# One-hot matrices by groups of 8 rows, two groups at a time, chunk innermost

## What is computed

```python
edge_index = jnp.stack([src, dst])
x = _layernorm(x + _L0_gnn_ref(x, src, dst, edge_weight, ...))   # relu(segment_sum(w * (x W)[dst], src) + b)
x = _layernorm(x + _L1_gnn_ref(x, edge_index, ...))              # 4-head attention over edges, softmax per dst
x = _layernorm(x + _L2_gnn_ref(x, ...))                          # attention over the same edges
x = _layernorm(x + _L3_gnn_ref(x, edge_index, ...))              # two mean aggregations over edges
```

## Time and profile before

| | us |
|---|---|
| median of 3 runs (2888.77 to 2893.41) | 2890.57 |
| profiled execution, its own time | 2890.26 |
| its span, first to last instruction | 2888.6 |
| edge tables, about | 0 to 66 |
| building of the matrices, about | 66 to 888 |
| the four layers | 888 to 2889 |

### The profile page before, as it was taken

The page is one execution under the profiler, slowest core; times in us unless marked ns, Lnnn a source line. Parts: engine busy times, 40 slices in busy tenths (PEclk is TensorE's granted clock), DMA queues, the critical chain, the costliest instruction groups (busy, mean ns, idle before and its releaser), DMA issues. The chain is left out here.

```text
span 2888.6 us, 62252 instructions
## 1 busy us (share of the span) xinstructions
PE 2395.0 (83%) x16954; PEld 1630.4 (56%) x16955; DVE 2073.9 (72%) x3472; ACT 1727.9 (60%) x4122; POOL 473.1 (16%) x825
## 2 busy tenths in 40 slices
PE   1898999889988958888888888888739999959795
PEld 1444444445544546666666666666617888835453
DVE  6776777777771025999999999999467888566075
ACT  1898999999992015766677777666426666410101
POOL 0444444444441000000000000000000000001010
PEclk7999999999999978999999999999869999979897
DMA  1222222222227801222222222222123333058193
GB/s 40 96 102 99 104 98 104 104 101 107 100 103 291 303 18 74 73 87 92 93 93 93 93 93 93 93 93 72 53 82 125 113 121 129 3 247 344 46 426 126
DMA packets 132234, 341.18 MB, mean 118 GB/s; under 512 B 13957, under 2 KB 114936, under 8 KB 115704
## 3 DMA queue, kind: packets, MB, share of 16 engines
q1 hardware_dynamic: 131960, 338.62, 31.5%
HBM read 212.41 MB, written 126.18 MB: 117 GB/s over the span
## 5 line engine op out<-in xcount | busy, mean ns | idle before, releaser
L434 PE MATMUL ps_build<-OH,KEY 128*128 128x400 bf16 x4108 | 737.4, 339 | 82.9 <-ACT KEY L391 47.2
L391 ACT ACTIVATE KEY<-KEY,cols 128x128 bf16<-128x128 bf16 x2054 | 621.7, 397 | 101.1 <-DVE KEY L362 100.0
L434 PEld LDWEIGHTS ps_build<-OH,KEY 128*128 128x128 bf16 x4108 | 399.8, 99 | 420.9 <-DVE OH L366 85.9
L1078 ACT ACTIVATE exponentials<-gr_ps,att_cols 128x256 f32<-128x256 f32 (+1 forms) x1300 | 499.5, 487 | 192.9 <-PE gr_ps L972 190.6
L362 DVE TENSOR_SCALAR KEY<-iota_key,key_base,cols 128x128 bf16<-128x128 int16 x1027 | 389.9, 412 | 220.9 <-PE ps_build L434 193.8
L409 POOL TENSOR_TENSOR KEY<-KEY,cols 128x256 bf16<-128x256 bf16 (+1 forms) x627 | 376.5, 601 | 499.6 <-DVE KEY L362 499.6
L972 PE MATMUL gr_ps<-ident,gr_r 128*128 128x128 f32 x2500 | 382.0, 292 | 84.3 <-DVE gr_r L1186 67.4
L1193 DVE SCALAR_TENSOR_TENSOR exponentials<-exponentials,gr_count_t 128x3072 f32<-128x3072 f32 (+1 forms) x104 | 349.4, 3360 | 54.2 <-ACT gr_count_t L1095 37.6
L1001 PE MATMUL gr_ps<-exponentials,heads 128*33 128x128 f32 x5000 | 366.1, 278 | 26.7 <-DVE exponentials L1193 26.7
L972 PEld LDWEIGHTS gr_ps<-ident,gr_r 128*128 128x128 f32 x2500 | 283.9, 147 | 168.7 <-issue 135.5
L1159 DVE CUSTOM_DVE_ANT_0 gr_unread<-gr_src_rows,gr_closed 128x3125 bf16<-128x3125 f32 (+1 forms) x100 | 344.1, 3441 | 13.5 <-ACT gr_closed L1071 12.9
(11 more groups left out here) (273 smaller groups left out, 1976.6 us busy)
## 6 DMA issues: line engine op xcount, KB each, us to landing
adjacency<-stage SPq DMA_DIRECT2D x200, 400.0 KB, 2.5
sage_ring<-count_by_source SPq DMA_DIRECT2D x50, 1600.0 KB, 9.2
agg_gcn_ring<-adjacency SPq DMA_DIRECT2D x25, 1600.0 KB, 8.3
gr_count<-adjacency SPq DMA_DIRECT2D x25, 1600.0 KB, 7.8
ar_counts<-adjacency SPq DMA_DIRECT2D x25, 1600.0 KB, 6.7
count_by_source<-gr_count_t SPq DMA_DIRECT2D x12, 3200.0 KB, 18.8
fg_node<-gat_node_sums SPq DMA_DIRECT2D x1, 1650.0 KB, 6.3
count_by_source<-gr_count_t SPq DMA_DIRECT2D x1, 1600.0 KB, 7.1
```

What stands on the lines that cost most here:

```text
L391: last = act.activation(KEY[:, slot + j, v, :], KEY[:, slot + j, 0, :], ACT.Copy, scale=k.cols[:, 1 + v, bass.ds(c + j, 1)])
L434: last = pe.matmul(ps[:, 2 * (s % 2) + (v > 0), 0:SL], KEY[:, slot + j, v, :], OH[:, slot + j, :], start=slot == s % 2 * (BODY + 1) and j ...
L1078: last = act.activation(e[:, s, 0:w], ps[:, i % RINGS, c:c + w], ACT.Exp, bias=cols[:, h, s:s + 1])
```

## The change

WD becomes 8 and SL 200, so a window has 8 rows x 16 slabs = 128 keys, and there are 400 windows. They are done two at a time: 200 pairs. A window's body is 3 chunks, a pair's six (BOTH). Buffers have four slots of a pair (RING), guarded the same way at each pair, and the loop has 50 laps of four.

- POOL no longer multiplies. It gathers, for each pair, the six chunks' keys (less the window's base), low parts and two weight parts as bf16 into `near`, and the third weight part as fp32 into `last_w`: three instructions for each window.
- VectorE makes KEY for all six chunks in one tensor_tensor of 128 x 6 against a grid, OH in one of 200 x 6, and then multiplies KEY by the first and second weight part, in two more. The chunk is the innermost index of all of them: KEY is [P, RING, 4, 128, 6].
- ScalarE multiplies by the third part, in six ACTIVATEs that read and write every sixth element, and copies four banks of 200 columns.
- TensorE's matmuls have 200 columns, and read KEY and OH with a step of six elements. Four a chunk, as before.
- A window's fourth chunk, and any behind it, go to a single extra slot, made wholly by VectorE behind its branch; TensorE takes it between the pair's first four chunks and its last two.
- SyncE stores counts and weights apart, in two DMAs a pair.
- `edge_tables` makes the slab number with three instructions instead of seven, the ranges of 400 windows with 28 steps instead of 42, and POOL writes two grids.

The core of the diff:

```diff
-WD = 16
+WD = 8
 NW = NP // WD
-SL = CW
+SL = CW // 2
-STEPS = ((0, 2), (2, 2), (4, 1))
-BODY = 5
-UW = 10
-LAG = 4
+QUARTERS = 4
+QW = NW // QUARTERS
+BODY = 3
+BOTH = 2 * BODY
+PAIRS = NW // 2
+RING = 4
+PLANES = 4
...
-            step(dve.tensor_scalar(hi[:], src[:], float(SL), None, ALU.is_ge))
-            for s in range(2, NSH):
-                step(dve.scalar_tensor_tensor(hi[:], src[:], float(SL * s), hi[:], ALU.is_ge, ALU.add))
+            step(dve.tensor_scalar(hi[:], src[:], 1.0 / SL, 0.5 / SL - 0.5, ALU.mult, ALU.add))
+            step(dve.tensor_scalar(hi[:], hi[:], ROUNDING, None, ALU.add))
+            step(dve.tensor_scalar(hi[:], hi[:], -ROUNDING, None, ALU.add))
...
+        @block.gpsimd
+        def _(pool):
+            def gather(q, u, words):
+                pool.wait_ge(used, q + 1)
+                for i in range(2):
+                    first = first_of(pool, words[i])
+                    mine = slice(i * BODY, (i + 1) * BODY)
+                    pool.tensor_tensor(near[:, u, 0, mine], k.cols[:, 0, bass.ds(first, BODY)],
+                                       k.key_base[:, bass.ds(q * 2 + i, 1)].to_broadcast([P, BODY]), ALU.subtract)
+                    pool.tensor_copy(near[:, u, 1:PLANES, mine], k.cols[:, 1:PLANES, bass.ds(first, BODY)])
+                    last = pool.tensor_copy(last_w[:, u, mine], k.cols[:, PLANES, bass.ds(first, BODY)])
+                last.then_inc(gathered, 1)
...
+            def onehots_of(q, u, words):
+                keys_wide, lows_wide = [P, P, BOTH], [P, SL, BOTH]
+                dve.wait_ge(gathered, q + 1)
+                dve.tensor_tensor(KEY[:, u, 0], k.key_grid[:], near[:, u, 0, :].unsqueeze(1).to_broadcast(keys_wide),
+                                  ALU.is_equal).then_inc(keys, 1)
+                dve.tensor_tensor(OH[:, u], k.low_grid[:], near[:, u, 1, :].unsqueeze(1).to_broadcast(lows_wide),
+                                  ALU.is_equal).then_inc(onehots, 1)
+                dve.wait_ge(keys, q + 1)
+                for v in range(1, PLANES - 1):
+                    last = dve.tensor_tensor(KEY[:, u, v], KEY[:, u, 0],
+                                             near[:, u, 1 + v, :].unsqueeze(1).to_broadcast(keys_wide), ALU.mult)
+                last.then_inc(parts, 1)
...
+            def last_part(q, u, lap):
+                act.wait_ge(keys, q + 1)
+                for j in range(BOTH):
+                    last = act.activation(KEY[:, u, PLANES - 1, :, j], KEY[:, u, 0, :, j], ACT.Copy,
+                                          scale=last_w[:, u, j:j + 1])
+                last.then_inc(last_parts, 1)
+                copy_out((u - 1) % 2, q, lap * (16 * RING) + 32 * (u // 2 + 1))
...
+                def body(i, j):
+                    for v in range(PLANES):
+                        last = pe.matmul(ps[:, bank(i, v), 0:SL], KEY[:, u, v, :, i * BODY + j], OH[:, u, :, i * BODY + j],
+                                         start=j == 0 and v < 2, stop=True, skip_group_check=True)
+                    return last
```

More of the change, by code:

```diff
@@ new lines, in beyond_body @@
+        def beyond_body(eng, word, ahead, work):
+            before = eng.snap(word >> SHIFT)
+            end = ahead >> SHIFT
+            with eng.If(before < end):
+                work(before, before)
+                with eng.If(before + 1 < end):
+                    with eng.Fori(before + 1, end) as at:
+                        work(at, before)
+        @block.gpsimd
+        def _(pool):
+            def gather(q, u, words):
+                pool.wait_ge(used, q + 1)
+                for i in range(2):
+                    first = first_of(pool, words[i])
[5 more added lines that the diff above has]
+                last.then_inc(gathered, 1)
+            each_pair_of_words(pool, gather)
@@ L386, in window @@
-            def window(lap, s, before, first, end):
-                def last_parts(slot, n, at, c, again=False):
-                    act.wait_ge(keys, at + n)
-                    for j in range(n):
-                        for v in (2, 3):
-                            last = act.activation(KEY[:, slot + j, v, :], KEY[:, slot + j, 0, :], ACT.Copy,
-                                                  scale=k.cols[:, 1 + v, bass.ds(c + j, 1)])
-                    last.then_inc(parts, n)
-                    if slot % (BODY + 1) == LAG:
-                        copy_out((s - 1) % 2, before, lap * (8 * UW) + 16 * (s // 2 + 1))
-                each_step(act, s, before, first, end, last_parts)
@@ L400, in _ @@
-            each_window(act, window)
-            total = act.value_load(k.table[0:1, NW:NW + 1], min_val=0, max_val=MAX_WORD)
-            copy_out(1, total >> SHIFT, 8 * NW + 16)
-        @block.gpsimd
-        def _(pool):
-            def window(lap, s, before, first, end):
-                def first_part(slot, n, at, c, again=False):
-                    pool.wait_ge(keys, at + n)
-                    pool.tensor_tensor(KEY[:, slot:slot + n, 1, :], KEY[:, slot:slot + n, 0, :],
-                                       k.cols[:, 2, bass.ds(c, n)].unsqueeze(2).to_broadcast([P, n, P]), ALU.mult
-                                       ).then_inc(first_parts, n)
-                each_step(pool, s, before, first, end, first_part)
-            each_window(pool, window)
+                act.activation(stage[:, slot].rearrange("p v i c -> p (v i) c"), ps[:, 4 * slot:4 * slot + 4, 0:SL], ACT.Copy).then_inc(copied, 1)
@@ L441, in _, with products, bank, more @@
-            each_window(pe, window)
+            def products(q, u, words):
+                def bank(i, v):
+                    return 4 * (u % 2) + 2 * (v > 0) + i
+                def body(i, j):
[3 more added lines that the diff above has]
+                    return last
+                pe.wait_ge(copied, q + 1)
+                pe.wait_ge(onehots, q + 1)
+                pe.wait_ge(parts, q + 1)
+                pe.wait_ge(last_parts, q + 1)
+                for i in range(2):
+                    for j in range(BODY - 1):
+                        body(i, j)
+                for i in range(2):
+                    def more(at, before):
+                        pe.wait_ge(more_made, at + 1)
+                        for v in range(PLANES):
+                            last = pe.matmul(ps[:, bank(i, v), 0:SL], more_key[:, v, :], more_oh[:], start=False, stop=True,
+                                             skip_group_check=True)
+                        last.then_inc(more_used, 1)
+                    beyond_body(pe, words[i], words[i + 1], more)
+                for i in range(2):
+                    last = body(i, BODY - 1)
+                last.then_inc(used, 1)
```

224 lines of the change are left out of this document (106 added, 118 removed).

## The result

The changed kernel takes 3385.36 us (median of 4 runs, 3384.94 to 3385.47) against 2891.13 (4 runs, 2888.77 to 2893.41) for the kernel before. The ratio is 1.1709, with a 95% interval of 1.1689 to 1.173. The forecast was 2693, its range 2600 to 3060: wrong in sign, and outside its range on the slow side.

The account below looks back on a forecast made before the run. TensorE at 2.95 us a pair, nearly level with VectorE plus POOL, was taken to bound matrix building: 200 x 2.95 + 32 + 3 = 625 against 819.9, -195, and -2 for tables: 2890 - 197 = 2693 us, range 2600 to 3060.

Parts of the forecast that it names:

- TensorE's price for elements 12 bytes apart: Matrix building, matmuls of 200 columns: 0.085 + 0.038 = 0.123 us each, 2.95 us a pair, ends 0.085 and 0.237.
- strided reads slow TensorE by the row's full price: Rival on matrix-building matmuls: 0.237 us each, 5.7 us a pair, whole kernel about 3236 us; chance 0.18.
- half-rate rival: TensorE at one column in two cycles, by stride or 1.2 GHz clock: 4.05 us a pair, 2899 us; chance 0.14.
- Forecast 0.50: Chance given to the likeliest case: matrix building at 2.47 to 3.2 us a pair, whole kernel 2600 to 2750 us.
- rival of 0.96 us: VectorE makes products and one-hots at one element a cycle: 4.73 us a pair, 3057 us; chance 0.10.
- ScalarE's strided product: ScalarE's six ACTIVATEs a pair, 12 bytes apart: 0.19 ns an element extra, 2.62 us a pair with the copy.
- POOL's small instructions: Six small POOL gathers a pair in matrix building, taken at 0.13 us each, their own length.
- VectorE's instruction stretched by POOL: POOL instructions do not run free beside VectorE; the small ones lengthen its path by 0.13 us each.
- 0.78 us put on VectorE's path: POOL's six small instructions a pair, added to VectorE's 2.12 us; ends 0 and 1.1 us.
- the lap stalls go: Matrix-building loop: stalls at lap heads vanish, since every pair has the same guard, four slots deep.
- 2.90 for VectorE and POOL: Matrix-building pace of VectorE with POOL: 2.12 + 0.78 = 2.90 us a pair, sharing the lead with TensorE at 2.95.
- middle case: POOL's loads and gathers, or ScalarE's strides and waits, make 3.3 to 3.9 us a pair: 2750 to 2870 us; chance 0.08.

Follow-up runs that it names:

- The experiment with one step for each chunk: Changed kernel with weights read packed and the moving operand at steps of 1 to 6 elements for the six chunks; wrong sums; 2881 us, one run.
- the first experiment: Changed kernel with TensorE reading both KEY and OH from neighbouring elements; wrong sums; 2768 us, one run, stage 700.6 us.
- the kernel without words: Kernel with three groups of two chunks; VectorE and TensorE read no table words and test for no fourth chunk, these left out; 2592 us, one run.
- the kernel with steps of two: Changed kernel with the six chunks laid out as three groups of two, pair innermost, so a matmul's step is 4 bytes; 2765.11 us, 0.9562 of before.
- half of the words: Kernel with three groups of two chunks; VectorE and TensorE read one table word and make one test a pair, not two; 2632.28 us, 0.9107 of before.

## Why the prediction was wrong, point by point

**The step that failed** is TensorE's price for elements 12 bytes apart, the term 0.038 us of its 0.123 us a matmul. It had the right row, 0.76 ns an element at 24 bytes, and from it an upper end of 0.237 us. It then divided by two twice, because a matmul streams one operand and because the distance is half, and took 0.123. Measured: 0.269. Neither halving had a row behind it. The experiment with one step for each chunk shows that the time does go with the distance, but as the whole time of the matmul (0.11 us a kilobyte spanned) and not as a small addition to it: TensorE's 0.085 us for 200 columns hide a step of two elements and nothing more. Even the upper end was too low by 0.032 us a matmul. The row was of fp32 elements 24 bytes apart on another engine, whose own pace of 1.04 ns an element may cover part of the distance; then its surplus could not bound TensorE from above. Its whole time, 1.04 + 0.76 = 1.8 ns an element, is the 1.8 ns that 16 bytes cost TensorE, as if each element had entered one piece of 16 bytes. That is an argument from two numbers and was not tried. (The packed row beside it is a product and not a subtraction, as the prediction has it.)

**The rival that came true** is "strided reads slow TensorE by the row's full price". It named the mechanism and the view that would show it, TensorE without gaps at over 0.13 us a matmul, and gave 3236 us. The rest is the size: 6.45 - 5.7 = 0.75 us a pair, 200 x 0.75 = 150 of the 149 us missing. It had a chance of 0.18 and lay outside the range. The half-rate rival had the clock at the 1.2 GHz level as a possible cause; the clock did fall to 0.50, and cost nothing at that step.

**The chance** was set wrong too. The text gave ends of 0.085 and 0.237 for the bounding engine, ends worth 2.6 against 5.7 us a pair, and wrote that no row settled them. With nothing near the taken value, "Forecast 0.50" was not earned by rows, and leaving out the one end that the only strided row gave made the range too short.

**Right, as the trace shows.** VectorE's products of 768 take 552 ns (0.56 forecast) and its one-hot of 1200 778 (0.785): 0.52 ns an element between the two, half of the fp32 row's 1.04, so the rival of 0.96 us is out. Matrix building remained the only stage that moved, the tables gave 2.5 us (2 forecast), and 108 = 27 x 4 matmuls of fourth chunks were made.

**Wrong in size, and hidden by TensorE.** ScalarE's strided product: 0.315 forecast, 0.389 at most, 0.41 measured, 3.44 us a pair, which alone would have made the kernel about as fast as the first experiment, 2768. POOL's small instructions: their own 0.14 us apart was right (0.13), but "VectorE's instruction stretched by POOL" was not; VectorE's stay at medians of 549 to 559 ns, and in the kernels that keep them close together it is POOL's that grow from 0.19 to 0.52 us and more beside a VectorE instruction. Of the 0.78 us put on VectorE's path, 0.2 to 0.5 is left in the kernel without words, and nothing in the kernel with steps of two.

**A term that was missing.** The forecast asked only whether POOL's table reads were doubtful, and said "the lap stalls go". In the kernel with steps of two, reads and tests on TensorE and VectorE cost 0.6 us a pair. The pace of 2.91 us within its laps lies beside the forecast's 2.90 for VectorE and POOL by chance, since POOL was some 4 us or more ahead there, and the pace fell to 2.3 with half of the words. Nor did the forecast have the ring of ScalarE and TensorE: its lower bound of 2.47 us a pair was ScalarE alone, where the ring holds 2.60. And the middle case's upper end was added up wrong, 200 x 3.9 + 32 + 3 = 815 against 819.9 makes 2883 and not 2870, which touches nothing else. Lap stalls, which I had laid to the slots' guard of the kernel before, come back with the same guard at every pair, 1.2 us in each of 50 laps. How much of the 92 us of stalls in the kernel before was of this kind wasn't tried.

## What to carry to other kernels

When a change puts another index innermost, write down for every reader the distance between its elements, and count TensorE's moving operand by the bytes spanned: here 200 bf16 columns cost nothing extra up to 4 bytes and 3.2 times as much at 12. An operand that one engine wants interleaved and another packed can often be interleaved by two, which kept VectorE's whole gain. Where no engine is full, look at the idle time put down to "issue", and at the register instructions in it: one table word and one test for each pair instead of two were worth 133 us of 2765. Before you write a loop out further, count its instructions: eight pairs in a lap for four cost 51 us. And add up the ring of two engines that wait for each other, not only each engine's own work.

## What the runs showed of the hardware that I had not expected

- TensorE's moving bf16 operand, 200 columns: 0.085, 0.09, 0.14, 0.175, 0.22, 0.27 us at steps of 1 to 6 elements; weights at a step of 6 cost 29 ns a load and 16 us of a stage of 4800 matmuls.
- A matmul held up by its reads takes 0.27 us at a granted clock of 0.50 as at 1.00, and the clock stood at 0.50 through a stage in which TensorE's rows show it busy 1315.7 of 1324 us.
- ScalarE, 128 bf16 read and written 12 bytes apart: 0.80 us long and 0.41 apart, against 0.39 and 0.29 packed; 4 bytes apart 0.42 and 0.30.
- A table word read into a register cost VectorE 0.73 us, of which the profile counts none as busy.
- Behind the branch to the loop's head VectorE waited for its code for 0.25 us in laps of 314 instructions and for 3.0 in laps of 622 and 1546; POOL for 0.2 in laps of 98 and 190 and for 2.6 in laps of 466; TensorE for 0.06 in all.
